# A decoder layer's self-attention stage: bias folding, split of the transposed input, one operation for four, order of transposes

## What is computed

```python
qkv = jnp.einsum('tbe,fe->tbf', query, qkv_w) + qkv_b
q, k, v = jnp.split(qkv, 3, axis=-1)
q = q * scaling
...
attn_weights = jnp.einsum('ntd,nsd->nts', q, k)      # 16 heads of 32, causal mask
attn_probs = jax.nn.softmax(attn_weights, axis=-1)
attn = jnp.einsum('nts,nsd->ntd', attn_probs, v)
out = jnp.einsum('tbe,fe->tbf', attn, out_w) + out_b
```

## Time and profile before

| | us |
|---|---|
| median of 3 runs | 2046.49 (2044.66 to 2046.70) |
| span of the profiled execution | 2039.5 |
| TensorE busy in it | 1831.5 |
| VectorE busy | 1619.9 |
| GpSimd busy | 1132.6 |
| ScalarE busy | 962.4 |

### The profile page before, as it was taken

The page is one execution under the profiler, slowest core; times in us unless marked ns, Lnnn a source line. Parts: engine busy times, 40 slices in busy tenths (PEclk is TensorE's granted clock), DMA queues, the critical chain, the costliest instruction groups (busy, mean ns, idle before and its releaser), DMA issues.

```text
span 2039.5 us, 35482 instructions
## 1 busy us (share of the span) xinstructions
PE 1831.5 (90%) x11712; PEld 1505.8 (74%) x11712; DVE 1619.9 (79%) x2427; ACT 962.4 (47%) x3070; POOL 1132.6 (56%) x858
## 2 busy tenths in 40 slices
PE   5789989999899899884899999999999999999994
PEld 4667777777777777763788888787887878878873
DVE  6598888888888888895578888787887878878875
ACT  4222221112222222201577777676776767767772
POOL 0387777777777777786354445433553435534432
PEclk8899999999999999996999999999999999999997
DMA  6101111111111111012011111011101111011101
GB/s 239 56 1 42 42 42 42 41 41 41 41 41 41 41 41 38 24 58 83 22 39 49 54 54 58 19 54 50 59 27 45 54 55 59 18 55 54 34 22 42
DMA packets 70224, 97.71 MB, mean 48 GB/s; under 512 B 5952, under 2 KB 29632, under 8 KB 70080
## 3 DMA queue, kind: packets, MB, share of 16 engines
q1 hardware_dynamic: 68208, 94.12, 14.1%
q10 hardware_dynamic: 1872, 1.66, 0.3%
HBM read 58.80 MB, written 36.96 MB: 47 GB/s over the span
## 4 chain that ended last, share of the span: by engine, by line
PE 43%; DVE 6%; issue 2%; ACT 2%; POOL 1%; DVEq 0%; POOLq 0%; ACTq 0%
PE ring L1114 21%; PE sc L1133 9%; PE ring L1160 4%; PE ring L1202 3%; PE sc L1136 3%; PE ring L1119 3%; DVE x2T L1279 2%; DVE x L1369 1%; ACT x2T L1212 1%; DVE q L1400 1%; ACT q L1212 1%; DVE g_sb L1295 1%; DVE stats_c L1350 1%; ACT prob_c L1239 0%; DVE vare_c L1376 0%
## 5 line engine op out<-in xcount | busy, mean ns | idle before, releaser
L506 PE MATMUL qb<-wqkv,xT 128*128 128x512 f32 x2304 | 556.6, 398 | 8.0 <-DVE qk L688 5.7
L506 PEld LDWEIGHTS qb<-wqkv,xT 128*128 128x128 f32 x2304 | 433.4, 191 | 109.4 <-DVE qk L688 12.6
L1239 ACT ACTIVATE prob_c<-sc,ntop 128x128 f32<-128x128 f32 x1024 | 361.8, 390 | 122.5 <-DVE ntop L1312 122.0
L1068 POOL TENSOR_TENSOR rstd<-vare,half_c 128x1 f32<-128x1 f32 x64 | 35.0, 546 | 472.0 <-DVE vare L1326 472.0
L600 ACT ACTIVATE aT<-tb 128x512 fp32r<-128x512 f32 x64 | 36.7, 590 | 473.3 <-PE tb L514 473.2
L1133 PE MATMUL sc<-kbd,q 128*128 128x512 f32 x768 | 230.9, 410 | 18.3 <-issue 16.7
L1239 ACT ACTIVATION_READ_ACCUMULATOR prob_c<-sc,ntop 128x1 f32 x1024 | 234.9, 229 | 0.0
L584 PE MATMUL ob<-wout,aT 128*128 128x512 f32 x768 | 201.2, 413 | 34.6 <-DVE aT L764 32.7
L1114 PE MATMUL ring<-wqkv,aT_c 128*128 128x512 f32 x768 | 195.0, 403 | 3.0 <-DVE x L1333 3.0
L584 PEld LDWEIGHTS ob<-wout,aT 128*128 128x128 f32 x768 | 146.5, 197 | 67.8 <-DVE aT L764 22.5
L1312 DVE TENSOR_REDUCE ntop<-sc 128x4 f32<-128x512 f32 x256 | 170.5, 685 | 29.2 <-PE sc L1136 22.8
(11 more groups left out here) (129 smaller groups left out, 3495.3 us busy)
## 6 DMA issues: line engine op xcount, KB each, us to landing
x_tile<-in_x SPq DMA_DIRECT2D x16, 1024.0 KB, 7.3
x_scratch<-xres SPq DMA_DIRECT2D x16, 1024.0 KB, 5.2
x_tile<-x_scratch SPq DMA_DIRECT2D x16, 1024.0 KB, 6.3
out<-x SPq DMA_DIRECT2D x64, 256.0 KB, 2.0
kbd<-k_scratch SPq DMA_DIRECT2D x64, 128.0 KB, 3.0
v_c<-v_scratch SPq DMA_DIRECT2D x16, 256.0 KB, 2.8
raw<-in_wqkv SPq DMA_DIRECT2D x3, 1024.0 KB, 17.3
ctx<-in_ctx SPq DMA_DIRECT2D x1, 1024.0 KB, 8.1
```

What stands on the lines that cost most here:

```text
L506: last = nc.tensor.matmul(qb[g % 4][:, :], xT[p][a][:, k, t * P:(t + 1) * P], wqkv[b][:, k, c * D:(c + 1) * D], start=(n == 0), stop=(n == ...
L1239: last = nc.scalar.activation(prob[:, h, :], sc[g][:, (h % 4) * C:(h % 4 + 1) * C], ACT.Exp, bias=ntop[:, h:h + 1], accum_out=total[:, t % ...
```

## The change

- The bias of v is no longer added to v. As the softmax weights of a row add up to 1, it passes through the attention unchanged, so its product with the output weights is added to the output bias, once, in `prepare_block` (12 matmuls of the replicated bias with `wout`).
- `x_lo` moves from GpSimd to VectorE and reads the bank `tb` itself; `xT_raw` and its copies go. GpSimd's step ends with `rstd`.
- The four subtractions of the softmax become one operation over all rows, and so do the four multiplications of `softmax_norm`.
- TensorE's order after P7 is new: `attn_T(0)`, P8, `attn_T(1)`, `xn_T(0)`, OP0, P9, `xn_T(1)`, `attn_T(2)`, OP1, P10, `xn_T(2)`, `attn_T(3)`, OP2, P11, `xn_T(3)`, OP3. The eight transposes of a step alternate between the two banks (`TB_TURNS`), each waiting for the low part of the one two turns back.
- ScalarE makes `xn` before `a_hi(0)`; VectorE does `nmr` before `scores(1)`, `take_qk(2)` and `take_qk(3)` earlier, `softmax_top` later.

The hunks left out rename semaphores, drop `xT_raw`, and declare and load the two parts of the bias.

```diff
--- before.py
+++ after.py
@@ -91,6 +91,9 @@
 STAGES = 4
 
 
+TB_TURNS = [("a", 0), ("a", 1), ("x", 0), ("x", 1), ("a", 2), ("x", 2), ("a", 3), ("x", 3)]
+
+
 def prepare_block(nc, x_in, ctx_in, mask_in, w_in, b_in, scratch, keep):
 
     with ExitStack() as stack:
@@ -206,16 +212,28 @@
                     if m == DK - 1:
                         last.then_inc(v_trans, 1)
 
+            pe.wait_ge(bv_lo, 1)
+            pe.wait_ge(w_lo, len(pieces))
+            pe.wait_ge(kvt_sb, 2 * DK)
+            n = 0
+            for k in range(DK):
+                for a, b in PASSES:
+                    last = nc.tensor.matmul(ps[0][:, :], bvrep[a][:, k, :], wout[b][:, k, :],
+                                            start=(n == 0), stop=(n == 11))
+                    n += 1
+            last.then_inc(bv_psum, 1)
+
         @block.scalar
         def _(act):
             act.dma_start(mask8[:, :], mask_in.rearrange("b c -> (b c)").rearrange("(o n) -> o n", o=1).to_broadcast([P, R * C])
                           ).then_inc(in_mask, 16)
             for i, name in enumerate(("bk", "bv")):
                 act.dma_start(bkv[:, i, :], b_in[name]).then_inc(in_bkv, 16)
-            act.dma_start(bqkv[:, :], b_in["bqkv"].rearrange("(o n) -> o n", o=1).to_broadcast([P, 3 * D])
+            act.dma_start(bqkv[:, :], b_in["bqk"].rearrange("(o n) -> o n", o=1).to_broadcast([P, 2 * D])
                           ).then_inc(in_bias, 16)
             act.dma_start(bout[:, :], b_in["bout"].rearrange("(o n) -> o n", o=1).to_broadcast([P, D])
                           ).then_inc(in_bias, 16)
+            act.dma_start(bvs[:, :], b_in["bvs"]).then_inc(in_bias, 16)
 
             def split_hi(n):
                 act.wait_ge(in_raw[n % STAGES], 16 * (n // STAGES + 1))
@@ -280,8 +298,12 @@
             dve.wait_ge(mask_inv, 1)
             dve.wait_ge(fill_ready, 3)
             nc.vector.tensor_scalar(maskfill[:, :], mask[:, :], fill[:, 0:1], None, ALU.mult).then_inc(mask_rows, 1)
-            dve.wait_ge(in_bias, 32)
+            dve.wait_ge(in_bias, 48)
             nc.vector.tensor_scalar(bqkv[:, 0:D], bqkv[:, 0:D], SCALE, None, ALU.mult).then_inc(bias_ready, 1)
+            nc.vector.tensor_copy(bvrep[0][:, :, :], bcast(bvs[:, :], P)).then_inc(bv_hi, 1)
+            dve.wait_ge(bv_hi, 1)
+            nc.vector.tensor_tensor(bvrep[1][:, :, :], bcast(bvs[:, :], P), bvrep[0][:, :, :].bitcast(F32),
+                                    ALU.subtract).then_inc(bv_lo, 1)
 
             for m in range(DK):
                 if m + 4 < len(pieces):
@@ -299,6 +321,8 @@
                 dve.wait_ge(v_h, r + 1)
                 nc.vector.tensor_tensor(vparts[:, r, 1, :], pv[r][:, :], vparts[:, r, 0, :],
                                         ALU.subtract).then_inc(v_l, 1)
+            dve.wait_ge(bv_psum, 1)
+            nc.vector.tensor_tensor(bout[:, :], ps[0][:, :], bout[:, :], ALU.add).then_inc(bout_ready, 1)
 
 
 def self_block(nc, x_in, x1_dram, w_in, keep):
@@ -437,24 +460,6 @@
                 pool.wait_ge(attn_pool, 2 * a + t - 1)
 
             def step(j, p):
-                def x_lo(t):
-
-                    if not has(j, 1):
-                        return
-                    tok = slice(t * P, (t + 1) * P)
-                    wait(pool, xt_raw, R * (j + 1) + t + 1)
-                    nc.gpsimd.tensor_tensor(xT[1 - p][1][:, :, tok], xT_raw[:, t % 2, :, :],
-                                            xT[1 - p][0][:, :, tok].bitcast(F32),
-                                            ALU.subtract).then_inc(xt_lo, 1)
-
-                def v_bias(t):
-
-                    if not has(j):
-                        return
-                    wait(pool, v_raw, R * j + t + 1)
-                    nc.gpsimd.tensor_tensor(v[:, t, :], v[:, t, :], bqkv[:, 2 * D:3 * D],
-                                            ALU.add).then_inc(v_sb, 1)
-
                 if has(j, -1):
                     weigh(j - 1, 2)
                 if has(j):
@@ -475,15 +480,6 @@
 
                     wait(pool, xn_done, R * (j + 1))
                     nc.gpsimd.tensor_tensor(rstd[:, :], vare[:, :], half[:, :], ALU.pow).then_inc(rstd_done, 1)
-                x_lo(0)
-                v_bias(0)
-                v_bias(1)
-                x_lo(1)
-                v_bias(2)
-                x_lo(2)
-                x_lo(3)
-                v_bias(3)
-
             nc.gpsimd.memset(half[:, :], -0.5).then_inc(consts, 1)
             pool.wait_ge(consts, 1)
             run_steps(pool, step, TILES)
@@ -517,6 +513,15 @@
 
             def step(j, p):
 
+                def turn_free(n):
+
+                    kind, t = TB_TURNS[n - 2] if n >= 2 else TB_TURNS[n + 6]
+                    at = j if n >= 2 else j - 1
+                    if kind == "a":
+                        wait(pe, at_lo, R * (at - 1) + t + 1) if has(at, -1) else None
+                    else:
+                        wait(pe, xt_lo, R * (at + 1) + t + 1) if has(at, 1) and not is_step(at, -2) else None
+
                 def attn_T(t):
 
                     if not has(j, -1):
@@ -526,48 +531,35 @@
                         wait(pe, attn_dve, 2 * a + t + 1)
                     else:
                         wait(pe, attn_pool, 2 * a + t - 1)
-                    if t < 2 and has(j):
-                        wait(pe, xt_raw, R * j + t + 3)
-                    elif t < 2:
-                        wait(pe, at_lo, R * (a - 1) + t + 3)
-                    elif t == 2:
-                        wait(pe, at_lo, R * a + 1)
-                    elif has(j, 1):
-                        wait(pe, xt_raw, R * (j + 1) + 1)
-                    else:
-                        wait(pe, at_lo, R * a + 2)
-                    transpose_row((0, 1, 0, 1)[t], attn, t).then_inc(at_psum, 1)
+                    n = TB_TURNS.index(("a", t))
+                    turn_free(n)
+                    transpose_row(n % 2, attn, t).then_inc(at_psum, 1)
 
                 def xn_T(t):
 
                     if not has(j, 1):
                         return
                     wait(pe, xn_done, R * (j + 1) + t + 1)
-                    if t == 2:
-                        wait(pe, xt_raw, R * (j + 1) + 2)
-                    elif has(j, -1):
-                        wait(pe, at_lo, R * (j - 1) + (2, 3, 0, 4)[t])
-                    elif t == 3:
-                        wait(pe, xt_raw, R * (j + 1) + 1)
-                    else:
-                        wait(pe, xt_raw, R * j + 4 - t)
-                    transpose_row((1, 0, 0, 1)[t], xn, t).then_inc(xt_psum, 1)
-
-                for g in range(9):
+                    n = TB_TURNS.index(("x", t))
+                    turn_free(n)
+                    transpose_row(n % 2, xn, t).then_inc(xt_psum, 1)
+
+                for g in range(8):
                     products(j, p, g)
                 attn_T(0)
+                products(j, p, 8)
+                attn_T(1)
+                xn_T(0)
+                output_projection(j, 0)
                 products(j, p, 9)
-                attn_T(1)
-                output_projection(j, 0)
+                xn_T(1)
                 attn_T(2)
-                xn_T(0)
+                output_projection(j, 1)
                 products(j, p, 10)
-                xn_T(1)
-                output_projection(j, 1)
+                xn_T(2)
                 attn_T(3)
+                output_projection(j, 2)
                 products(j, p, 11)
-                xn_T(2)
-                output_projection(j, 2)
                 xn_T(3)
                 output_projection(j, 3)
 
@@ -608,11 +600,8 @@
                     if t == 0:
                         wait(act, qkv_psum, N_QKV * j)
                     wait(act, xt_psum, R * (j + 1) + t + 1)
-                    bank = tb[(1, 0, 0, 1)[t]][:, :]
+                    bank = tb[TB_TURNS.index(("x", t)) % 2][:, :]
                     nc.scalar.activation(xT[1 - p][0][:, :, tok], bank, ACT.Copy).then_inc(xt_hi, 1)
-                    wait(act, xt_lo, R * (j + 1) + t - 1)
-                    nc.scalar.activation(xT_raw[:, t % 2, :, :].rearrange("p k n -> p (k n)"), bank,
-                                         ACT.Copy).then_inc(xt_raw, 1)
 
                 def take_v(t):
 
@@ -639,7 +628,6 @@
                             last = nc.scalar.activation(whi, staging, ACT.Copy)
                     last.then_inc(w_hi, 1)
 
-                a_hi(0)
                 split_hi(0)
                 split_hi(1)
                 if has(j, 1):
@@ -651,17 +639,18 @@
                     for t in range(R):
                         nc.scalar.activation(xn[:, t, :], x[1 - p][:, t, :], ACT.Identity, bias=nmr[:, t:t + 1],
                                              scale=rstd[:, t:t + 1]).then_inc(xn_done, 1)
-                a_hi(1)
+                a_hi(0)
                 split_hi(2)
                 split_hi(3)
-                a_hi(2)
+                a_hi(1)
+                take_v(0)
                 x_hi(0)
```

(72 more changed lines are left out.)

1 line of the change is left out of this document (removed).

## The result

The changed kernel takes 2143.8 us (median of 4 runs) against 2045.6 us: 1.048 times the time before, interval 1.047 to 1.050. That is 98 us slower, where 95 were forecast. The profiled execution spans 2144.9 us, 105 more than that of before.

A forecast was written before the change was run, and what follows sets the result against it. The self stage was taken as bound by a closed loop through GpSimd's chain, not by TensorE. Longer laps (56.9), last lap (6.1), first chain (-0.9) and restarts (33.6) gave +95.7, rounded to 95: 2141 us, range 2100 to 2164.

The forecast's parts named there:

- Rival B: Self stage: the order sets GpSimd and VectorE apart, shortening GpSimd's chain; faster, 2013 us at 22.2 us; chance 0.06.
- Rival C: Self stage: VectorE joins the bound, adding 1 to 1.5 us a lap, 2155 to 2162 us; chance 0.14.
- Term (c): TensorE's new order: OP0, P9 and one more set of transposes stand behind `xn_T(0)`, +6.05 us on the loop.
- (a): `x_lo` and `v_bias` leave GpSimd: off the loop, 0; VectorE takes on 2.6 us a lap.
- (b): Softmax subtraction and normalisation in one operation each, 0.42 us: subtraction off the loop, 0; normalisation -0.21 us.
- (d): ScalarE's `a_hi(0)` behind `xn`: `nmr` to `xn_T(0)` stays 4.57 us, bounds 0 to +0.6.
- (e): VectorE's `nmr` ahead of `scores(1)`: its 5.35 us wait costs nothing extra; GpSimd's chain falls from 29.90 to 29.0 us.
- Term (f): TensorE's clock: a slow restart after the pause in every lap, 2.4 us each, fourteen making 33.6 us.
- Rival A: TensorE's clock: the longer loop without slow restarts, low clock passing during the pause; +62, 2109 us; chance 0.15.

The follow-up runs named there:

- fill46: The changed kernel with 46 matmuls of no use put ahead of `xn_T(0)` on TensorE; 2104.0 us, 1.029 of before.
- rstd_early: The changed kernel with `rstd` ahead of `weigh(3)` on GpSimd; 2048.6 us, 1.002 of before.
- p9_first: The changed kernel with P9 ahead of `xn_T(0)` again on TensorE, OP0 staying behind; 2109.7 us, 1.032 of before.
- xres_last: The changed kernel with the four `xres` behind `rstd` on GpSimd; 2081.5 us, 1.018 of before.
- new_order_only: The kernel before with only the change's orders on TensorE, ScalarE and VectorE and its bank turns; 2135.8 us, 1.045 of before.
- fill: The changed kernel with 36 matmuls of no use put ahead of `xn_T(0)` on TensorE; 2121.9 us, 1.037 of before.
- old_order: The changed kernel with the old orders put back, `x_lo` kept on VectorE; 2068.6 us, 1.012 of before.
- new_short: rstd_early with `nmr` right behind `scores(0)` and `x_hi(0)` ahead of `take_v(0)`; 2058.6 us, 1.007 of before.
- old_order_rstd: old_order with `rstd` ahead of `weigh(3)` on GpSimd and nothing else; 1994.9 us, 0.976 of before.
- short_loop: old_order_rstd with `nmr` behind `scores(0)` and `a_lo`, `scores(2)`, `scores(3)`, `x_lo(2)`, `softmax_top` moved in VectorE's list; 1962.2 us, 0.960 of before.

## Why the prediction was right

**The bound.** That the closed loop `nmr`, `xn`, `xn_T(0)`, OP3, `softmax_norm`, GpSimd's chain, `rstd` bounds the self stage of the changed kernel is shown three times over: by more work on TensorE that makes the kernel faster (fill46), by one call moved on GpSimd that gives 95 us back (rstd_early), and by the group-wise gain of p9_first. Rival B needed a chain under 24.6 us; it is 29.0. Rival C's extra 1 to 1.5 us a lap are absent: the clean lap is 58.4.

**Term (c), the order.** From `xn_T(0)` to the end of OP3 the sum had 22.02 us; fill46 shows 21.85 at full clock (727.91 to 749.76). The 0.17 is what is left of two errors in the prices, which were one size for all: a product group right behind an output group takes 2.73 us (731.15 to 733.88 in fill46) and not 2.845, and of two sets of transposes in a row the first takes 0.43 and not 0.35.

**Terms (a), (b), (d), (e).** The chain is 29.01 (forecast 29.0), `take_x1(3)` to GpSimd 2.60 (2.60), `nmr` to `xn_T(0)` 4.56 (4.57), the fused operations 0.42 each (0.42). The subtraction fell from 2.23 to 0.42 us and that gained nothing, as it is off the loop. Clean lap: 4.56 + 21.85 + 0.20 + 2.60 + 29.01 + 0.12 = 58.34.

The sum used what the page "SBUF — State Buffer" of the Trainium skill says of VectorE and GpSimd blocking each other (section "SBUF: two separate sides") only to weigh rival B. The runs agree with it: where an instruction of two SBUF inputs was moved beside GpSimd's, it grew, as `nmr` from 0.16 to 0.90 us in xres_last.

**Term (f), the clock.** Mis-sized: 2.4 us assumed, 1.98 measured on average, between 1.3 and 2.9 from lap to lap (687.84 to 711.09 less 21.85 is 1.40). It is still right that every lap pays. Rival A, no restart, would have been fill46's lap; its 58.4 is what A described, and the changed kernel's is 60.36.

**Where the total hides errors.** Between the `xn_T(0)` the laps make 13 x (60.36 - 54.12) = 81.1 us, where 88.1 had been summed. The first `xn_T(0)` comes 1.9 us later (141.87 to 143.79), where 0.9 earlier was forecast. Three delays show at the start of the stage: the preparation ends 0.8 us later, the first `nmr` runs beside `xres` and takes 1.21 us for 0.16, and TensorE's transposes of the first tile now wait for `x_lo` one by one. And from the last `xn_T(0)` to `kbd` it takes 117.0 us against 104.7: 12.3, where one longer way and one restart made 8.5. Of the missing 3.8, 3.7 lie in step 15, which has no `xn` (from the end of step 14's OP3 to step 16's `attn_T(0)` it takes 58.98 us, 952.57 to 1011.55, against 55.29 before):

```profile
977.52 0.60 PE L510 MATMUL tb<-ident,attn 128*128 128x128 f32 x4
980.51 4.61 PE L576 MATMUL ob<-wout,aT 128*128 128x512 f32 x12 [2.39 <-DVE aT L751]
```

P9 now stands behind OP0, so TensorE comes to OP0 after nine product groups and not ten, one group (2.8 us) earlier, while VectorE ends `a_lo(0)` as late as before: 27.9 us behind the end of the last OP3 (952.57 to 980.45), against 28.1 (861.43 to 889.53). TensorE waits 2.39 us for it and restarts slowly. The prediction hadn't looked at the steps at the edge of the pipeline. 81.1 + 1.9 + 12.3 = 95.3: three errors of -7.0, +2.8 and +3.8 cancel, so the agreement with 95.7 to the microsecond is luck; the agreement of the lap's parts is not. The measured 98 holds a fourth: the sum had nothing for the cross-attention, where the two profiled executions differ by 10.0 us. Their spans differ by 105 and the medians by 98, because the execution of before was a quick one (some 4 us under its median) and that of after lies 2.9 above its own.

**The cross-attention.** Behind the self stage the profiled executions need 1089.4 us (before), 1086.3 (new_order_only), 1090.2 (fill), 1087.0 (fill46), but 1099.4 (after), 1097.6 (old_order), 1096.8 (p9_first), 1096.1 (xres_last), 1096.9 (rstd_early), 1096.4 (new_short), 1100.8 (old_order_rstd) and 1097.9 (short_loop), with the same instructions. That is up to 14.5 us, in two groups. The four short ones are two kernels with unfolded bias and `x_lo` on GpSimd and two with the whole change and the added matmuls, so neither the change nor its absence alone decides. From 6 us behind the start of that part to the end the granted clock is 0.97 in before, new_order_only and fill, and 0.96 in after, old_order and xres_last, so the longer ones had a little more low clock. What causes it is left open; no kernel here was made to find out.
